# The masked cross-attention of a two-layer perceiver, written anew in the form of its sister, with fp32 probabilities and values

## The chip, the cores and the metric

The kernel runs on 1 core of one Trainium2 chip. The metric is the device time of one execution in microseconds (us). All six phases of the model are one program on that core: masked cross-attention (x0), a state-space layer (m0), a quantised feed-forward layer (f0), a sigmoid cross-attention (x1, here "the sister"), self-attention (a1) and routed experts (e1).

## What is computed

There are 128 batches of 32 tokens, width 256, and for each batch a context of 257 rows of width 256. The change touches the first phase only, whose reference is:

```python
q = _split_heads(query @ Wq + bq, B)
k = _split_heads(key @ Wk + bk, B)
v = _split_heads(value @ Wv + bv, B)
scores = jnp.einsum('bhqd,bhkd->bhqk', q, k) / np.sqrt(D_K)
scores = jnp.where(mask[:, None, :, :] > 0, NEG, scores)
p = jax.nn.softmax(scores, axis=-1)
x = jnp.einsum('bhqk,bhkd->bhqd', p, v)
x = x.transpose(0, 2, 1, 3).reshape(B, -1, D_MODEL)
return x @ Wo + bo
```

There are 16 heads of 16 columns; the query is the layer-normed residual stream, key and value are the context, the mask is int32 of shape 128 x 32 x 257, and NEG is -1e9. The result is added to the residual.

## The kernel before

The residual stream (4096 tokens x 256, fp32) stays in SBUF as `all_xres`, 32 tiles of 128 tokens. A tile is a **group** of four batches (`GB = 4`, `NT = 32` groups). The function `cross_attention` (L179) serves x0 alone (`soft` is true); the sister has a function of its own, `sigmoid_attention` (L976), which isn't touched.

An fp32 operand of a product is mostly kept as two fp16 tiles, hi and lo (hi is the value rounded, lo the rest), and `mm_split` makes three fp16 matmuls of one product: hi x hi, lo x hi, hi x lo (L263 is the line of all its matmuls, L1147 that of the sister's). In tile names h and l at the end are these halves; `x_psK`, `x_psV`, `x_psS`, `x_psT`, `x_psO` and `x_psM` are PSUM tiles for keys, values, scores, transposed probabilities, attention output and small things (psA, a part of psM, serves transposed queries, queries and output projection in turn).

What each engine does for a batch slot c (the numbers in brackets are lags, which keep the engines apart):

- **PE**: the transposes of batch c-2's probabilities, eight fp32 transposes of 128x128 (L464); values of c, twelve matmuls of 256 columns; scores of c, twelve of 256 columns over all 128 rows (the queries stand in a block-diagonal tile, `x_qbd`) and twelve of one column for context row 257; keys of c+1, twelve of 256 columns; then attend of c-2, 24 fp16 matmuls in 64-column tiles, and more for row 257. Once in four batches each: transposed and projected queries, keys and values of row 257, output projection.
- **DVE**: `softmax_max` (L843, four custom instructions that add the mask and take the row maximum, then `x_nm`, L846), the reciprocals of the row sums (L852), the lo halves of keys (L882), values (L890) and probabilities (L861, twice), extraction of the heads from psO, conversion of the mask (`to_add`, L829), the layer norm's last step (L174).
- **ACT**: four exponentials with row sums (L705), the hi halves of probabilities (L676), values (L697), keys (L689) and queries (L659).
- **POOL**: normalises the probabilities (L376, four a batch), splits the context in hi and lo (L346, L348), spreads the queries into `x_qbd` by a head mask of 8 columns (L356), copies row 257 (L332, L336), adds the output bias (L367).
- **SP** issues the loads: for each group the context (L299, 128 x 2056 fp32) and behind it four copies of the mask (L305).

The order of work is written by hand: every engine has its own loop over the batches, in program order, and engines meet in semaphores. An instruction whose semaphore isn't up holds everything behind it on its engine. Buffers: context 2 (a group each), keys 2, values 4, probabilities 2, transposed probabilities 1, mask int32 1 and converted 2.

Of the kernel before, what the change touches and what calls it, by code (L numbers as in the profile page):

```python
# [6 lines left out]
F32 = mybir.dt.float32  # L7
# [5 lines left out]
ALU = mybir.AluOpType  # L13
# [165 lines left out]
def cross_attention(nc, d, xres, con, norm, layer):  # L179

    soft = layer == 0
    with ExitStack() as ctx:
        sp = Space(nc, ctx, f"x{layer}")
        sb, ps, sem = sp.sb, sp.ps, sp.sem
        pre = f"L{layer}_xattn_"

        W = {k: (sb(f"w{k}h", [P, C, D], F16), sb(f"w{k}l", [P, C, D], F16)) for k in "qkvo"}
        begin_layer(nc, f"x{layer}w", xres, norm, [(d[pre + "W" + k], *W[k], WS) for k in "qkvo"])
        bq, bk, bv = (sb(f"b{k}", [P, C], F32) for k in "qkv")
        bo = sb("bo", [P, D], F32)
# [12 lines left out]
        V = [(sb(f"vh{n}", [P, C, 256], F16), sb(f"vl{n}", [P, C, 256], F16)) for n in range(4)]
        kx = [(sb(f"kxh{n}", [P, C, GB], F16), sb(f"kxl{n}", [P, C, GB], F16)) for n in range(2)]
        xk = (sb("xkh", [P, C, 96], F16), sb("xkl", [P, C, 96], F16))
        vx3 = sb("vx3", [96, D], F16)  # L210
        vxm = [sb(f"vxm{n}", [96, GB, D], F16) for n in range(2)]

        NP = 2
        prob = [sb(f"prob{n}", [P, 4, S2], F32) for n in range(NP)]
        pT32 = sb("pT32", [P, 4 * 256], F32) if not soft else None
        mx = [sb(f"mx{n}", [P, 4], F32) for n in range(2)]
        nm = [sb(f"nm{n}", [P, 4], F32) for n in range(2)]
        sm = [sb(f"sm{n}", [P, 4], F32) for n in range(2)]
        rs = [sb(f"rs{n}", [P, 4], F32) for n in range(2)]
        pT = [(sb(f"pTh{n}", [P, 2, 512], F16), sb(f"pTl{n}", [P, 2, 512], F16)) for n in range(1 if soft else 2)]  # L220
        px = [sb(f"px{n}", [P, 96], F32) for n in range(2)]
        px3 = sb("px3", [96, P], F16)

        oT = [sb(f"oT{n}", [P, GB, C, T], F32) for n in range(2)]
        ob = sb("ob", [P, C, P], F32)
        obp = (sb("obh", [P, C, P], F16), sb("obl", [P, C, P], F16))
# [3 lines left out]
        psA = psM[:, 0:256]  # L230
        psX = psM[0:96, 256:384]
        psKx = psM[:, 384:392]
        psSx = psM[:, 392:408]
        score = [psS, psS] if soft else [psS, psT]
        SC = 0.25 / (WS * WS)
        PXS = 1.0 if soft else PS

        const_in, bias_ready, px_zeroed = sem("const_in"), sem("bias_ready"), sem("px_zeroed")
        ctx_in = [sem(f"ctx_in{n}") for n in range(2)]
        mask_in, mask_used = sem("mask_in"), sem("mask_used")  # L240
        pool_passed, sync_passed = sem("pool_passed"), sem("sync_passed")
        ctx_hi, ctx_split, xk_hi, xk_ready = sem("ctx_hi"), sem("ctx_split"), sem("xk_hi"), sem("xk_ready")
# [3 lines left out]
        vx_mm, vx_hi, vx_lo, vxm_ready = sem("vx_mm"), sem("vx_hi"), sem("vx_lo"), sem("vxm_ready")  # L246
        k_mm, k_hi, k_lo = sem("k_mm"), sem("k_hi"), sem("k_lo")
        v_mm, v_hi, v_lo = sem("v_mm"), sem("v_hi"), sem("v_lo")
        s_mm, sx_taken, s_max, nm_ready, dve_passed = (sem(k) for k in ("s_mm", "sx_taken", "s_max", "nm_ready", "dve_passed"))
        exp_done, r_ready, p_norm = sem("exp_done"), sem("r_ready"), sem("p_norm")  # L250
        p_main = sem("p_main")
        t_mm, pt_hi, pt_lo, pv_mm = sem("t_mm"), sem("pt_hi"), sem("pt_lo"), sem("pv_mm")
        pxT_mm, px_hi, px_lo, o_full = sem("pxT_mm"), sem("px_hi"), sem("px_lo"), sem("o_full")
        o_part, o_ext, ob_ready, ob_hi, ob_lo = sem("o_part"), sem("o_ext"), sem("ob_ready"), sem("ob_hi"), sem("ob_lo")
# [4 lines left out]
        def mm_split(eng, out, lhs, rhs, start, stop, lint=False):  # L259

            prods = [p for a, b in zip(lhs, rhs) for p in split_products(a, b)]
            for n, (a, b) in enumerate(prods):
                last = eng.matmul(out, a, b, start=start and n == 0, stop=stop and n == len(prods) - 1,  # L263
                                  skip_group_check=lint)
            return last

        def both(pair, f):
            return (f(pair[0]), f(pair[1]))

        LASTI = NT // 2 - 1

        def run(eng, body):
            for i in range(LASTI + 1):
                body(i)

        def preps(i, gp):

            return not (isinstance(i, int) and i == LASTI and gp == 1)  # L280

        def started(i, c, lag):

            return not (isinstance(i, int) and 8 * i + c - lag < 0)


        @block.sync
        def _(sync):
            if soft:
                for t, k in ((bq, "q"), (bk, "k"), (bv, "v")):  # L290
                    sync.dma_start(t[:], d[pre + "b" + k]).then_inc(const_in, 16)
                sync.dma_start(bo[:], d[pre + "bo"].rearrange("(a n) -> a n", a=1).to_broadcast([P, D]))\
                    .then_inc(const_in, 16)

            def load(i, gp):
                g = i * 2 + gp
                wait_apart(sync, ctx_split, (g - 1) * GB, sync_passed)
                wait_apart(sync, xk_ready, g - 1, sync_passed)
                sync.dma_start(ctx32[gp][:], d["ctxT"][bass.ds(g, 1)].rearrange("a p j c s -> (a p) j c s"))\  # L299
                    .then_inc(ctx_in[gp], 16)  # L300
                if soft:
                    wait(sync, mask_used, g)
                    src = d["mask"][bass.ds(g * GB, GB)].rearrange("j q k -> q j k")
                    for h in range(4):
                        sync.dma_start(mraw[32 * h:32 * h + 32], src).then_inc(mask_in, 16)  # L305

            def body(i):
                for gp in range(2):
                    load(i, gp)
# [2910 lines left out]
```

## Time and profile before

| | before |
|---|---|
| median of 3 runs | 3196.28 us |
| the runs | 3201.59, 3191.54, 3196.28 us |
| the profiled execution | 3201.86 us |
| its span | 3200.1 us |
| mean granted TensorE clock | 0.923 of full |
| PE, DVE, ACT, POOL busy over the span | 85%, 72%, 60%, 60% |
| instructions | 85879 |

The span is the time from the first to the last record of the profile; the profiled execution is 1.8 us longer. The shares are means over six phases with different limits, so they say little of one phase; a window's row gives the same for a stretch of time. x0 lies between about 40 and 1045 us.

### The profile page before, as it was taken

To read this page: it belongs to the slowest core of one execution; us is meant where nothing else is said; L and a number is where in the kernel's file an instruction comes from. 1 tells how busy PE (TensorE), PEld (TensorE's weight loads), DVE (VectorE), ACT (ScalarE), POOL (GpSimd) and SP (SyncE) were. 2 spreads that over 40 slices of the span, in tenths; PEclk is the share of its full clock that TensorE was granted. 3 is DMA by queue.
4 is the path that set the end of the run, shared out by engine and by line. 5 is a ranking of instruction groups with operands and counts; after the bars stand their busy time and mean duration, and the time that the engine had idled before them with its cause. 6 is when DMAs were issued, how large, how long until landed. Compare 5 with 4: busy or idle time off the path is not lost. (4 is left out here: it accounts for less than half of the span.)

```text
span 3200.1 us, 85879 instructions
## 1 busy us (share of the span) xinstructions
PE 2706.9 (85%) x32700; PEld 2118.3 (66%) x32700; DVE 2312.3 (72%) x5209; ACT 1905.3 (60%) x4534; POOL 1931.9 (60%) x2135
## 2 busy tenths in 40 slices
PE   3999999999998489998677999999995788546998
PEld 2877777777777355555344788888884666434776
DVE  4999999999998387777634677777775788663443
ACT  2666767676666577767233677777773666343333
POOL 4888788888885477777300766666662677233332
PEclk9999999999999688988688999999997999757999
DMA  5121111111110000000000221111210000352110
GB/s 144 42 61 61 42 61 50 53 61 42 61 48 2 20 1 1 1 1 1 14 16 16 93 61 57 53 59 61 61 47 16 2 2 2 121 182 74 38 38 28
DMA packets 87375, 143.57 MB, mean 45 GB/s; under 512 B 10784, under 2 KB 74144, under 8 KB 80704
## 3 DMA queue, kind: packets, MB, share of 16 engines
q1 hardware_dynamic: 82304, 123.52, 12.4%
q0 software_dynamic: 4672, 14.57, 1.3%
q8 instruction: 270, 4.42, 0.6%
q14 instruction: 129, 1.06, 0.1%
HBM read 123.37 MB, written 14.69 MB: 43 GB/s over the span
## 5 line engine op out<-in xcount | busy, mean ns | idle before, releaser
L376 POOL TENSOR_SCALAR x_prob<-x_prob,x_rs 128x257 f32<-128x257 f32 x512 | 247.8, 484 | 173.1 <-DVE x_rs L852 141.6
L705 ACT ACTIVATE x_prob<-x_prob,x_nm 128x257 f32<-128x257 f32 x512 | 254.3, 498 | 152.6 <-DVE x_nm L846 152.5
L2119 DVE TENSOR_TENSOR_SCAN m_s<-m_a,m_psD 128x1024 f32<-128x1024 f32 x128 | 284.9, 2267 | 2.3 <-PE m_psD L1946 2.2
L1420 DVE SCALAR_TENSOR_TENSOR x_pTl<-x_psS,x_pTh 128x1024 f16<-128x1024 f32 x128 | 156.7, 1225 | 145.3 <-ACT x_pTh L1328 145.3
L843 DVE CUSTOM_DVE_ANT_0 x_prob<-x_psS,x_masked,x_prob 128x256 f32<-128x256 f32 x512 | 217.3, 481 | 4.5
L2058 ACT ACTIVATE m_a<-m_dt,m_rate 128x248 f32<-128x248 f32 x512 | 206.8, 492 | 0.0
L1108 POOL TENSOR_TENSOR x_qbdh<-x_qh,all_mask4h 128x1024 f16<-128x1024 f16 x32 | 60.6, 1895 | 217.5 <-DVE x_ql L1401 217.5
L1830 POOL TENSOR_TENSOR m_s<-m_s 128x1024 f32<-128x1024 f32 x64 | 150.5, 2352 | 67.8 <-DVE m_s L2119 67.8
L3003 ACT ACTIVATE e1t_g<-e1t_psH,e1t_bias 128x128 f32<-128x128 f32 x312 | 89.2, 368 | 171.0 <-PE e1t_psH L2952 171.0
L689 ACT ACTIVATE x_kh<-x_psK,x_bk 128x256 f16<-128x256 f32 x256 | 107.5, 471 | 118.6 <-PE x_psK L263 116.1
L861 DVE TENSOR_TENSOR x_pTl<-x_psT,x_pTh 128x512 f16<-128x512 f32 x256 | 164.2, 682 | 5.6 <-ACT x_pTh L676 3.0
L1341 ACT ACTIVATE x_vh<-x_psV 128x512 f16<-128x512 f32 x128 | 76.4, 597 | 134.7 <-PE x_psV L1147 134.7
L1100 POOL TENSOR_TENSOR x_ctxl<-x_ctx,x_ctxh 128x512 f16<-128x512 f32 x128 | 149.7, 1170 | 10.7
L348 POOL TENSOR_TENSOR x_ctxl<-x_ctx,x_ctxh 128x512 f16<-128x512 f32 x128 | 144.1, 1125 | 10.7
L2952 PE MATMUL e1t_psH<-e1t_xnh,e_wh 128*128 128x128 f16 x624 | 143.2, 229 | 2.8 <-issue 2.2
L1147 PE MATMUL x_psK<-x_ctxh,x_wkh 128*128 128x256 f16 x512 | 142.0, 277 | 3.4 <-POOL x_ctxl L1100 3.1
L263 PE MATMUL x_psS<-x_kh,x_qbdh 128*128 128x256 f16 x512 | 140.5, 274 | 4.4 <-POOL x_qbdl L356 4.3
L1322 ACT ACTIVATE x_psS<-x_psS 128x1024 f32<-128x1024 f32 x128 | 129.0, 1008 | 24.2 <-PE x_psS L1241 24.2
L464 PE MATMUL x_psT<-all_ident,x_prob 128*128 128x128 f32 x1024 | 135.8, 276 | 6.5 <-POOL x_px L382 6.5
L1147 PE MATMUL x_psV<-x_wvh,x_ctxh 128*128 128x256 f16 x512 | 141.0, 275 | 0.0
L1147 PE MATMUL x_psK<-x_ctxh,x_wkl 128*128 128x256 f16 x512 | 140.7, 275 | 0.0
L1147 PE MATMUL x_psK<-x_ctxl,x_wkh 128*128 128x256 f16 x512 | 140.7, 275 | 0.0
(599 smaller groups left out, 11913.9 us busy)
## 6 DMA issues: line engine op xcount, KB each, us to landing
x_ctx<-in_ctxT SPq DMA_DIRECT2D x32, 1028.0 KB, 6.3
x_ctx<-in_ctxT SPq DMA_DIRECT2D x32, 1024.0 KB, 5.9
x_mraw<-in_mask SPq DMA_DIRECT2D x128, 128.5 KB, 2.8
e1r_stage<-in_L_ffn_w SPq DMA_DIRECT2D x16, 1024.0 KB, 5.0
e_rows<-e1r_pad POOLq DMA_DIRECT2D x1, 5070.0 KB, 19.6
e1t_row<-e_rows SPq DMA_DIRECT2D x39, 130.0 KB, 2.1
all_xres<-in_x SPq DMA_DIRECT2D x1, 4096.0 KB, 14.2
x_vxr<-x_vx SPq DMA_DIRECT2D x128, 32.0 KB, 3.4
```

The lines of the kernel that those rows point to most:

```text
L348: pool.tensor_tensor(lo[:, j], src, hi[:, j], ALU.subtract).then_inc(ctx_split, 1)
L376: last = pool.tensor_scalar(prob[n][:, h, :], prob[n][:, h, :], rs[n][:, h:h + 1], PS, ALU.mult, ALU.mult)
L705: last = act.activation(prob[n][:, h, :], prob[n][:, h, :], ACT.Exp, bias=nm[n][:, h:h + 1], scale=SC, accum_out=sm[n][:, h:h + 1])
L843: dve.tensor_tensor_reduce(prob[n][:, h, 0:256], psS[:, h * 256:(h + 1) * 256], masked[gp][:, j, 0:256], 1.0, prob[n][:, h, 256:257], ALU. ...
L861: dve.tensor_tensor(pT[0][1][:, kt, :], psT[:, kt * 512:(kt + 1) * 512], pT[0][0][:, kt, :], ALU.subtract).then_inc(pt_lo, 1)
L1100: pool.tensor_tensor(lo[:, j], src, hi[:, j], ALU.subtract).then_inc(ctx_split, 1)
L1147: last = pe.matmul(out, a, b, start=m == 0, stop=m == len(prods) - 1)
L1420: dve.scalar_tensor_tensor(pT[c % 4][1][:].rearrange("p r k n -> p (r k n)"), psS[c % 2][:], PS, pT[c % 4][0][:].rearrange("p r k n -> p ( ...
L1830: pool.tensor_tensor(lower, lower, upper, ALU.add).then_inc(half_done, 1)
L2058: last = act.activation(A[k % 3][:, :, m, 1:T], dt[n % 2][:, h, :].rearrange("p (j t) -> p j t", t=T)[:, :, 1:T], ACT.Exp, scale=rate[:, h ...
L2119: dve.tensor_tensor_scan(states, rates, psD[at % 2][:], 0.0, ALU.mult, ALU.add).then_inc(scan_done, 1)
L2952: last = pe.matmul(bank[:, k % 4 * P:(k % 4 + 1) * P], a, b, start=m == 0, stop=m == len(prods) - 1)
```

## The change

`cross_attention` is replaced by `masked_attention` (L179 of the changed kernel); the other phases are as before. Its parts:

- **Loads.** Per group: `load_vx` (values of row 257, from DRAM, broadcast over partitions, 128 x 1024 fp32), `load_mask` (four copies), `load` (context without its last row, 128 x 8 x 256 fp32), in this order on SP. `load_vx(g)` waits for the `value_last` of batch 4g-5.
- **Row 257.** Its keys and values are computed for all 128 batches at the start (`last_keys`), its values go through a DRAM tensor `x0_vx`. Its scores are made once a group (`last_scores`), turned into the last column of the probabilities by `last_values` (DVE) and `place_last` (POOL), and its part of the output comes from `value_last` (POOL, `x_pv`) and four fp32 matmuls with the identity.
- **Softmax.** `minima` (DVE) works on -SC times the scores and takes the minimum, which is the exponential's bias, so `x_nm` isn't computed apart. The exponentials are not normalised: the row sums are spread (`spread_sums`, POOL), added up by two fp32 matmuls (`denominators`, PE), and the group's output is multiplied by the reciprocals (`normalise`, DVE). `mask` conversion moves from DVE to POOL (`to_add`).
- **Scores** run in two tiles of 64 rows, with the 4-column head mask.
- **Probabilities and values stay fp32**: their copies out of PSUM are whole (ACT and DVE take half of pT each, ACT takes V) and `attend` makes 8 fp32 matmuls of 64 columns instead of 24 fp16 ones. The products with Wq, Wk, Wv, Wo and the scores stay split.
- Buffers: keys and values 4, probabilities and transposed probabilities 3. Keys are made two batches ahead, attend lags by two.

The diff, cut to its core:

```diff
-def cross_attention(nc, d, xres, con, norm, layer):
+def masked_attention(nc, d, xres, con, norm):
+    NK, NV, NP, NW = 4, 4, 3, 3
...
-            def load(i, gp):
-                g = i * 2 + gp
-                wait_apart(sync, ctx_split, (g - 1) * GB, sync_passed)
...
+            def load(g):
+                wait(sync, ctx_split, (g - 1) * GB)
+                sync.dma_start(ctx32[g % 2][:], d["ctxT"][g][:, :, :, 0:LAST]).then_inc(ctx_in[g % 2], 16)
+            def load_mask(g):
+                wait(sync, mask_done, g)
...
+            def load_vx(g):
+                wait(sync, pv_last, (g - 1) * GB)
...
+            for g in range(NT):
+                load_vx(g)
+                if g > 0:
+                    load_mask(g)
+                if g > 1:
+                    load(g)
...
+            def to_add(g):
+                pool.wait_ge(mask_in, 64 * (g + 1))
...
+                pool.tensor_scalar(masked[g % 2][:], mraw[:, :, 0:LAST], 0.0, -BIG, ALU.is_gt, ALU.mult).then_inc(mask_done, 1)
+            def value_last(b):
+                g, j = b // GB, b % GB
+                pool.wait_ge(exp_done, b + 1)
+                pool.wait_ge(vxr_in[g % 2], 16 * (g // 2 + 1))
+                wait(pool, pv_mm, b - 1)
...
+            for b in SLOTS:
+                g, j = b // GB, b % GB
+                batch(value_last, b - 1)
+                if j == 2:
+                    group(spread, g + 1)
+                batch(split, b + GB)
+                if j == 0:
+                    group(spread_sums, g - 1)
+                    group(to_add, g + 1)
+                if j == 1:
+                    group(add_bo, g)
+                batch(place_last, b + 1)
...
+            for b in SLOTS:
+                g, j = b // GB, b % GB
+                batch(scores, b)
+                if j == 0:
+                    group(output, g - 2)
+                batch(keys, b + 2)
+                if j == 1:
+                    group(queries, g + 1)
+                if j == 2:
+                    group(denominators, g - 1)
+                if j == 3:
+                    group(last_scores, g + 1)
+                batch(turn, b - 1)
+                batch(values, b)
+                if j == 0:
+                    group(xnT, g + 1)
+                batch(attend, b - 2)
...
+            def minima(b):
+                g, j = b // GB, b % GB
+                dve.wait_ge(placed, b + 1)
+                dve.wait_ge(s_mm, b + 1)
...
+            for b in SLOTS:
+                g, j = b // GB, b % GB
+                batch(minima, b)
+                if b % 2 == 0 and 0 <= b - 4 < NB:
+                    extract((b - 4) // 2)
...
+                batch(take_pT, b - 1)
+                if j == 1:
+                    group(lo_q, g + 1)
+                    group(ln, g + 2)
+                batch(lo_k, b + 2)
```

ACT's loop of the new layer is exps(b), take_pT(b-1), [hi_q in a group's second slot], hi_k(b+2), take_v(b).

How the order of instructions moves, first on SP, whose queue carries all loads. Before, at the steady state of the layer:

```order
L299 DMA x_ctx_0<-in_ctxT 128x2056 [waits x0_xk_ready,x0_ctx_split]
L305 DMA x_mraw<-in_mask 32x4x257 [waits x0_mask_used]
L305 DMA x_mraw<-in_mask 32x4x257 x3
L299 DMA x_ctx_1<-in_ctxT 128x2056 [waits x0_xk_ready,x0_ctx_split]
L305 DMA x_mraw<-in_mask 32x4x257 [waits x0_mask_used]
L305 DMA x_mraw<-in_mask 32x4x257 x3
```

And SP after, at the same place (`x0_pv_last` is raised by `value_last`):

```order
L293 DMA x_vxr<-x_vx 128x1024 [waits x0_pv_last]
L288 DMA x_mraw<-in_mask 32x4x257 [waits x0_mask_done]
L288 DMA x_mraw<-in_mask 32x4x257 x3
L282 DMA x_ctx_0<-in_ctxT 128x8x256 [waits x0_ctx_split]
L293 DMA x_vxr<-x_vx 128x1024 [waits x0_pv_last]
```

The context load was the first of its group and depends only on the context's own users; it is now the last, behind the load that waits for `x0_pv_last`.

POOL in the first slot of a group, before (`x_xkh` and `x_xkl` are the halves of context row 257):

```order
L332 CAST x_xkh<-x_ctx_1 128x3x16 [waits x0_vx_mm,x0_ctx_in1]
L332 CAST x_xkh<-x_ctx_1 128x3x16
L336 TENSOR_TENSOR x_xkl<-x_ctx_1,x_xkh 128x3x16 [waits x0_xk_hi]
L336 TENSOR_TENSOR x_xkl<-x_ctx_1,x_xkh 128x3x16
L346 TENSOR_SCALAR x_ctxh<-x_ctx_1 128x512 [waits x0_v_mm,x0_ctx_in1]
L348 TENSOR_TENSOR x_ctxl<-x_ctx_1,x_ctxh 128x512 [waits x0_ctx_hi]
```

POOL in the first slot of a group, after:

```order
L350 TENSOR_TENSOR x_pv_1<-x_vxr,x_prob 128x256 [waits x0_pv_mm,x0_vxr_in1,x0_exp_done]
L316 TENSOR_SCALAR x_ctxh<-x_ctx_1 128x512 [waits x0_v_mm,x0_ctx_in1]
L318 TENSOR_TENSOR x_ctxl<-x_ctx_1,x_ctxh 128x512 [waits x0_ctx_hi]
L358 TENSOR_TENSOR x_sums<-x_eye_q,x_sm 128x512 [waits x0_sum_mm,x0_exp_done]
L336 TENSOR_SCALAR x_mlast<-x_mraw 128x4 [waits x0_last_done,x0_s_min,x0_mask_in]
L337 TENSOR_SCALAR x_masked<-x_mraw 128x1024
L343 COPY x_prob<-x_lastv 128x4 [waits x0_pv_last,x0_t_mm,x0_last_done]
```

Before, the split of the next group's first batch (L346, L348) followed the copies of row 257, and the normalisations of the running batch came after it. It (L316, L318) now stands right behind the `value_last` (L350) that SP's queue waits for, and the mask conversion (L337) and `place_last` (L343) stand behind the split.

PE after, at the end of one slot and the start of the next (attend, then scores; keys follow, waiting for `x0_k_lo` and `x0_ctx_split`):

```order
L512 MATMUL x_psO<-x_pT,x_v 64x128 [waits x0_pv_last,x0_pt_second,x0_o_ext,x0_pt_first,x0_v_out]
L512 MATMUL x_psO<-x_pT,x_v 64x128 x7
L518 MATMUL x_psO<-all_ident,x_pv_0 64x128 x4
L485 MATMUL x_psS<-x_kh,x_qbdh 128x256 [waits x0_s_min,x0_k_lo]
L485 MATMUL x_psS<-x_kh,x_qbdh 128x256
L485 MATMUL x_psS<-x_kl,x_qbdh 128x256 x2
L485 MATMUL x_psS<-x_kh,x_qbdl 128x256 x2
L485 MATMUL x_psS<-x_kh,x_qbdh 128x256 x2
L485 MATMUL x_psS<-x_kl,x_qbdh 128x256 x2
L485 MATMUL x_psS<-x_kh,x_qbdl 128x256 x2
L395 MATMUL x_psK<-x_ctxh,x_wkh 128x256 [waits x0_k_lo,x0_ctx_split]
```

An attend is now twelve products of 128 columns into tiles of 64 columns, and scores twelve in tiles of 64 rows.

## Rows read from the trace of the kernel before

**Rows 1.** Windows, 500 to 600 us (us, PE PEld DVE ACT POOL busy, PEclk, DMA, GB/s)
```profile
500.00:600.00 100.00, 92.72 (x1211) 78.75 (x1210) 91.64 (x274) 70.13 (x219) 82.20 (x120) 1.00 0.18 57
```

**Rows 2.** Waits of 300 to 900 us (us in total, times, longest)
```profile
ACT x_prob L705 <- DVE x_nm L846: 95.8, 79, 1.9
```

**Rows 3.** Timeline of DVE, the layer's first and last maximum (start us, us)
```profile
59.10 0.49 DVE L843 CUSTOM_DVE_ANT_0 x_prob<-x_psS,x_masked,x_prob 128x256 f32<-128x256 f32 x1
...
1028.32 0.48 DVE L843 CUSTOM_DVE_ANT_0 x_prob<-x_psS,x_masked,x_prob 128x256 f32<-128x256 f32 x1
```

**Rows 4.** Timeline of PE in x0, transposes and values
```profile
507.41 1.04 PE L464 MATMUL x_psT<-all_ident,x_prob 128*128 128x128 f32 x8
...
508.29 0.27 PE L263 MATMUL x_psV<-x_wvh,x_ctxh 128*128 128x256 f16 x1
508.40 0.27 PE L263 MATMUL x_psV<-x_wvl,x_ctxh 128*128 128x256 f16 x1
```

**Rows 5.** Timeline of PE in the sister, the scores' first and the keys' first
```profile
2000.55 0.23 PE L1241 MATMUL x_psS<-x_qbdh,x_kh 64*128 64x128 f16 x2
...
2001.33 0.28 PE L1147 MATMUL x_psK<-x_ctxh,x_wkh 128*128 128x256 f16 x1
```

**Rows 6.** Timeline of PE in the sister, an fp32 product beside fp16 ones
```profile
1910.56 0.43 PE L1186 MATMUL x_psM<-x_qx,x_head_sum 128*64 128x128 f32 x2
1910.72 0.24 PE L1261 MATMUL x_psO<-x_pTh,x_vh 128*64 128x128 f16 x1
...
1910.83 0.27 PE L1186 MATMUL x_psM<-x_qx,x_head_sum 128*64 128x128 f32 x1
```

**Rows 7.** The page's costliest groups, two of POOL (busy us, mean ns | idle before)
```profile
L376 POOL TENSOR_SCALAR x_prob<-x_prob,x_rs 128x257 f32<-128x257 f32 x512 | 247.8, 484 | 173.1 <-DVE x_rs L852 141.6
...
L1108 POOL TENSOR_TENSOR x_qbdh<-x_qh,all_mask4h 128x1024 f16<-128x1024 f16 x32 | 60.6, 1895 | 217.5 <-DVE x_ql L1401 217.5
```

**Rows 8.** Timeline of POOL in x0
```profile
515.89 0.62 POOL L346 TENSOR_SCALAR x_ctxh<-x_ctx 128x512 f16<-128x512 f32 x1
516.59 1.16 POOL L348 TENSOR_TENSOR x_ctxl<-x_ctx,x_ctxh 128x512 f16<-128x512 f32 x1
517.71 0.73 POOL L367 TENSOR_TENSOR all_xres<-all_xres,x_bo 128x256 f32<-128x256 f32 x1
```

**Rows 9.** Timeline of SP, one group's masks and the next context
```profile
525.67 1.75 SPq L305 DMA_DIRECT2D x_mraw<-in_mask  x4
527.51 0.38 SPq L299 DMA_DIRECT2D x_ctx<-in_ctxT  x1
```

**Rows 10.** The line of the context load, L299, all 32
```profile
DMA to landing us min/median/max: 4.8/6.3/10.8
```

**Rows 11.** Timeline of ACT in x0
```profile
523.84 0.51 ACT L705 ACTIVATE x_prob<-x_prob,x_nm 128x257 f32<-128x257 f32 x1 [1.23 <-DVE x_nm L846]
...
525.83 0.60 ACT L659 ACTIVATE x_qh<-x_psM,x_bq 128x128 f16<-128x128 f32 x2
526.33 1.06 ACT L676 ACTIVATE x_pTh<-x_psT 128x512 f16<-128x512 f32 x2
...
528.95 0.84 ACT L689 ACTIVATE x_kh<-x_psK,x_bk 128x256 f16<-128x256 f32 x2 [1.07 <-PE x_psK L263]
```

**Rows 12.** DVE: lo_k of x0 in its timeline, the norm's step in x0 and the sister
```profile
61.97 0.88 DVE L882 SCALAR_TENSOR_TENSOR x_kl<-x_psK,x_bk,x_kh 128x256 f16<-128x256 f32 x2 [0.24 <-ACT x_kh L689]
...
L174 DVE TENSOR_SCALAR x_xn<-all_xres,all_mean,all_rstd 128x256 f32<-128x256 f32 x29 | 11.7, 403 | 0.0
...
L174 DVE TENSOR_SCALAR x_xn<-all_xres,all_mean,all_rstd 128x256 f32<-128x256 f32 x32 | 41.9, 1310 | 0.0
```

**Rows 13.** Timeline of PE in the state-space layer, and a window right behind it
```profile
1157.76 0.39 PE L1946 MATMUL m_psD<-m_bd1h,m_ut1h 32*128 32x512 f16 x2 [2.48 <-DVE m_s L2119]
...
1159.60:1163.00 3.40, 3.40 (x19) 1.77 (x17) 3.09 (x3) 3.33 (x8) 3.04 (x2) 0.50 0.00 0
```

More of the change, by code:

```diff
@@ L219, in cross_attention @@
[L219 to L226, printed above, removed]
+        (xnp,), (qp,) = parts("xn", [P, C, P], 1), parts("q", [P, C, P], 1)
@@ L232, in cross_attention @@
[L232 to L242, printed above, removed]
+        psA, psX = psM[:, 0:256], psM[:, 256:272]
@@ L257, in cross_attention @@
         block = ctx.enter_context(nc.Block())
[L259 to L268, printed above, removed]
@@ L272, in cross_attention, with batch, group @@
[L272 to L284, printed above, removed]
+        SLOTS = range(NB + 2 * GB)
+        def batch(f, b):
+            if 0 <= b < NB:
+                f(b)
+        def group(f, g):
+            if 0 <= g < NT:
+                f(g)
@@ L430, in xnT @@
+            def xnT(g):
                 pe.wait_ge(norm_tile.done, g + 1)
+                wait(pe, x_done, g - 2)
+                wait(pe, last_done, g)
                 for c in range(C):
@@ new lines, in _ @@
+            for h in range(C):
+                for r in range(RG):
+                    rows = slice(64 * r, 64 * r + 64)
+                    last = act.activation(kxp[0][rows, h, r, :], psK[rows, h * NB:(h + 1) * NB], ACT.Identity,
+                                          bias=bk[rows, h:h + 1])
+            last.then_inc(kx_hi, 1)
+            act.wait_ge(vx_mm, 1)
+            act.activation(vx32[:], psV[:, 0:D], ACT.Copy).then_inc(vx_done, 1)
+            hi_xn(0)
+            hi_k(0)
+            hi_q(0)
@@ new lines, in _ @@
+            last.then_inc(kx_lo, 1)
+            lo_xn(0)
+            ln(1)
+            lo_k(0)
+            lo_q(0)
+            lo_k(1)
+            last_values(0)
+            for b in SLOTS:
+                g, j = b // GB, b % GB
+                batch(minima, b)
+                if b % 2 == 0 and 0 <= b - 4 < NB:
+                    extract((b - 4) // 2)
+                if j == 0:
+                    group(residual, g - 2)
+                if j == 2:
+                    group(normalise, g - 1)
+                if j == 3:
+                    group(last_values, g + 1)
+                batch(take_pT, b - 1)
+                if j == 1:
+                    group(lo_q, g + 1)
+                    group(ln, g + 2)
+                batch(lo_k, b + 2)
+                if j == 0:
+                    group(lo_xn, g + 1)
+                if j == 3:
+                    group(lo_ob, g - 1)
```

891 lines of the change are left out of this document (322 added, 569 removed).

## The prediction

> **What bounds the kernel now.** I read the windows first: in 500 to 600 us, inside the rewritten layer, PE and DVE are both busy over 90% of the time and TensorE's clock is full (PEclk 1.00) [rows 1]. The waits of 300 to 900 us name the cycle that paces a batch: scores, DVE's four maxima, nm, then ACT's exponentials, whose wait for nm is the longest in the list [rows 2]. The DVE timeline gives the layer's length. The first maximum of batch 0 starts at 59.10 us, that of batch 127 at 1028.32 us [rows 3], so the masked layer takes 969.2 us between them: 7.63 us a batch, 30.5 us a group of four. The other phases keep their code. The whole question is the new layer's group period.
>
> **The change where PE would be the bound.** Twelve 256-column matmuls of keys or of values take 12 x 0.11 = 1.31 us (the starts in rows 4 are 0.11 apart), the eight fp32 transposes of `turn` 0.88 (507.41 to 508.29) [rows 4]. The change keeps these 32 products of a batch, since weights, queries and keys stay split into fp16 halves; only probabilities and values become fp32. New per batch:
> - Scores: 12 matmuls in two 64-row tiles, six pairs, instead of 12 full ones and 12 of one column. The sister's 12 pairs of half the columns take 2000.55 to 2001.33 = 0.78 us [rows 5]; with the switch back I take 0.88.
> - Attend: 12 fp32 matmuls of 64-column tiles. The sister has such an fp32 product: its passes appear as rows of their own, 0.27 us apart with an fp16 matmul of the other half between them, 0.11 after the first of them [rows 6]. So a product is two passes of about 0.11, and if the halves overlap, 24 passes take 12 x 0.11 = 1.32, with switches 1.52.
>
> A bare slot is 0.88 + 1.31 + 0.88 + 1.31 + 1.52 = 5.9 us. Once a group come the output projection 0.65 and the queries 0.65 (half of 1.31 each), two transposes 0.22, the denominators 0.84 (two overlapping fp32 products of 256 columns, 0.44, and a tile switch of 0.2 on either side) and the last scores, at most 0.6: 3.0. That makes 4 x 5.9 + 3.0 = **26.6 us a group**, in slots of 6.8, 6.55, 6.75 and 6.5. DVE loses nm, the reciprocals, half of each pT and V; its new normalisation comes once a group. ACT and DVE hide under 26.6, and POOL, without its four 0.484 us multiplications a batch [rows 7], would too: its new list is about 2.7 us a batch (steps 1 and 3 below) and, a group, two spreads of 1.9 [rows 7], spread_sums, conversion and an add, some 19 us in all. Costed at nothing: the `mlast` column, `normalise` (two DVE operations a group, where DVE has room), and the start's keys and values of row 257, against which the old group-wise ones go.
>
> **The wait it adds.** SP now issues vx, four mask copies and then the context, and the vx load waits for `value_last` of the batch before the group's first slot, b0. On POOL the instruction behind that `value_last` is the split of batch b0+4, which needs this very context. Behind it stand spread_sums, the mask conversion (moved from DVE) and `place_last(b0+1)`, for which the minima of b0+1 wait. `value_last(b0-1)` itself waits for attend(b0-3), which ends where slot b0 starts on PE; call that 0. The case comes 30 times (groups 2 to 31 are loaded so).
> 1. `value_last`: 0.1 + 0.73, the duration of the 128x256 add in rows 8; hand-over to SP: **1.0**.
> 2. vx issue about 0.45, four masks 1.84 (525.67 to 527.51 [rows 9]): the context is issued at 3.3. Landing: a median of 6.3 us [rows 10] for a 1.03 MB load with 0.51 MB behind it. Now 0.51 + 0.51 MB go ahead of 1.02 MB. Scaled by bytes the whole burst takes 6.3 x 2.05/1.54 = 8.4 us from its first issue, so I take 6.0 from the context's: **9.3**. Bounds for this step: 4.8 (its fastest) and 8.4.
> 3. Split 0.62 + 1.16 = 1.8; spread_sums 1.16 (same shape and kind) [rows 8]; mlast 0.2; conversion of 128x1024 int32 on POOL, which no row shows. The bounds: twice the 0.62 of a 512-element tensor_scalar = 1.24, and four times 0.484 = 1.94 [rows 7]; I take 1.7, since the int32 source is the dearer-looking kind. place 0.2. The minima of b0+1 start at **14.4**.
> 4. From there: first minimum 0.49 [rows 3]; four exponentials 1.99 (523.84 to 525.83); half of the two pT copies, 0.53; hi_q 0.60; hi_k 0.84 [rows 11]; lo_k 0.88 [rows 12]; hand-overs 0.1: 5.4, so lo_k(b0+3) is ready at **19.8**. psK has one buffer, so keys(b0+4) on PE wait for it.
>
> Without the wait these keys would start at 6.8 + 6.55 + 0.88 = 14.2. The stall is 5.6 us, in two pieces of about 2.8 around scores(b0+2). After it come 1.31 + 0.84 + 0.88 + 1.31 + 1.52 = 5.86 and slot three, 6.5: the next group's zero is at **32.2**.
>
> The clock: after 2.48 us idle in the state-space layer PE ran at 0.50, 1.2 instead of 2.4 GHz, for 3.4 us, starting 1.8 us later [rows 13]. That is 1.7 us of work lost. Two gaps longer than that one follow each other here; I take one such stretch a group, bounds 0 and 2.5. Period **33.9**.
>
> Between lo_q and lo_k DVE also has ln of group g+2. In this layer that row is 0.40 us and hides beside hi_k; in the sister the same instruction means 1.31 [rows 12]. I take 0.40; 1.31 would add 0.9 us a group, 27 in all, and is the upper bound. The Trainium skill (page "SBUF — State Buffer", section "Who interferes with whom") says that VectorE and GpSimd share a port pair under an exclusive lock, so that one can block the other's whole instruction. By that rule 3314 rather than 3287 if POOL's `spread`, released as lo_q ends, is first at the port; the trace's two means agree with the rule, not with a fixed price.
>
> The Trainium skill also gives, for the SWDGE path ("DMA: Bandwidth & Descriptors", section "Anatomy of one DMA — SWDGE (gpsimd) path"), about 2.0 us plus bytes/436e9 for one transfer. An estimate by it for 2.05 MB is 6.7 us instead of my 8.3, which would make the sum 1.6 x 30 = 48 us less, 3239; our queue is SP's, and the medians of rows 10 are slower than that formula.
>
> **The sum.** Group 0 26.6, thirty groups 33.9 each = 1017.0, three last slots 20.1: 1063.7 against 969.2, or +94.5. Head and tail: the pipeline drains one stage sooner, about -4, bounds -14 and +6. Together +90. The profiled execution took 3201.9, giving 3292; the median of the runs is 5.6 below the profiled one, so the forecast is **3287 us**.
>
> **The rivals.**
> - *The fp32 halves do not overlap.* No row shows two fp32 products side by side. Then attend is 1.32 dearer; in slots 0 and 1 the stall covers it, in 2 and 3 it is 2.64, and the denominators 0.43: 3.07 x 30 = 92, with some 10 for the groups without a stall: **3389**. Against it speaks the spacing in rows 6. Chance 0.10.
> - *The stall never reaches PE* (the other side). If the burst lands and POOL finishes before PE has used up its keys, 31 x 26.6 + 20.1 = 844.7, which is -124.5, with -4: **3068**. The place is keys(b0+4). It decides on the period: at (969.2 + 4 - 46.7)/30 = 30.88 us the change costs nothing, so stall and clock together must come to less than 4.3 of my 7.3 for any gain. Against it: all four steps are serial, and rows give most of them. Chance 0.14.
> - *My chain with its cheap ends.* Landing -1.2, conversion -0.46, no clock loss -1.7 give 30.5: just no change, 3187. The dear ends (+2.4, +0.24, +0.8, ln +0.9) give 38.2: 3417. This is inside my main case.
> - *Another wait*, such as attend's for `value_last` or psM's sharing between five users, chance 0.08, either sign.
>
> **How the numbers follow.** Main case 0.68, of which 0.06 is faster and 0.02 the same; no overlap 0.10, slower; hidden 0.14, faster; the rest 0.08: 0.02 faster, 0.01 same, 0.05 slower. Faster by over 0.3% 0.22, within 0.3% 0.03, slower 0.75; 0.3%, some 10 us, is about what measuring this kernel can tell from no change. The range is 3170 to 3400: from the cheap ends with the head's bound to the no-overlap case. It leaves out the hidden case and the farthest dear ends.
>
> **What would show it.** Right: POOL idle before the split's first instruction (`ctxh`) on the context's DMA, about 8 us, 30 times; PE idle before keys (on lo_k) and before scores (on the minima), near 5.6 us a group; PEclk below 1.00 in the layer's windows; DVE far below 92%. Attend's 24 passes within 1.5 us show the overlap. Wrong: the context landing before `value_last` ends, or PE near 100% with a period under 28 us; or attend near 2.8 us.

## The result, and the profile after

| | before | after |
|---|---|---|
| median | 3195.06 us (4 runs) | 3414.5 us (4 runs, 3409.01 to 3417.94) |
| ratio | 1 | 1.0683, 95% interval 1.066 to 1.0705 |
| the profiled execution | 3201.86 us | 3414.86 us |
| mean granted TensorE clock | 0.923 | 0.882 |
| PE, DVE, ACT, POOL busy | 85%, 72%, 60%, 60% | 80%, 59%, 53%, 52% |

The changed kernel is slower by 219 us where +90 was forecast: the sign and the mechanism were right, the size was not, and the time lies outside the range.

The waits of 300 to 900 us after the change, which answer to [rows 2] (us in total, times, longest):

```profile
ACT x_prob L579 <- DVE x_nm L666: 266.7, 63, 13.4
DVE x_prob L666 <- POOL x_prob L343: 192.5, 16, 12.7
POOL x_ctxh L316 <- DMA x_ctx<-in_ctxT: 167.4, 16, 11.2
...
PE x_psS L485 <- DVE x_nm L666: 112.0, 16, 7.7
...
PE x_psK L395 <- DVE x_kl L679: 32.5, 15, 2.2
```

These are the links of the predicted chain, all but the first once a group (16 groups fall into the stretch): POOL's split waits 10.5 us for the context, DVE's minima 12.0 for `place_last`, PE 7.0 for the minima and 2.2 for lo_k. So PE is idle 9.2 us a group; the forecast had 5.6.

One group on POOL, from its timeline (start, duration, and in brackets the idle time before):

```profile
586.14 0.62 POOL L316 TENSOR_SCALAR x_ctxh<-x_ctx 128x512 f16<-128x512 f32 x1 [11.03 <-DMA x_ctx<-in_ctxT]
586.84 1.15 POOL L318 TENSOR_TENSOR x_ctxl<-x_ctx,x_ctxh 128x512 f16<-128x512 f32 x1
587.95 1.07 POOL L358 TENSOR_TENSOR x_sums<-x_eye_q,x_sm 128x512 f32<-128x512 f32 x1
588.99 0.25 POOL L336 TENSOR_SCALAR x_mlast<-x_mraw 128x4 f32<-128x4 int32 x1
589.30 3.63 POOL L337 TENSOR_SCALAR x_masked<-x_mraw 128x1024 f32<-128x1024 int32 x1
592.99 0.19 POOL L343 COPY x_prob<-x_lastv 128x4 f32<-128x4 f32 x1
```

From the split to `place_last` it is 7.04 us instead of 5.1, and the difference is the mask conversion, 3.63 us where I took 1.7. Before, DVE did it (four columns more):

```profile
L829 DVE TENSOR_SCALAR x_masked<-x_mraw x32: 683/686/2380, 50.4 to 982.3; 128x1028 f32<-128x1028 int32 x32
```

One group on SP, behind a `value_last` that starts at 614.01:

```profile
614.66 0.34 SPq L293 DMA_DIRECT2D x_vxr<-x_vx  x1
615.05 1.86 SPq L288 DMA_DIRECT2D x_mraw<-in_mask  x4
616.95 0.55 SPq L282 DMA_DIRECT2D x_ctx<-in_ctxT  x1
```

The line of the context load, all 32, which answers to [rows 10]:

```profile
DMA to landing us min/median/max: 6.2/7.8/8.8
```

SP issues as predicted, at once when `value_last` ends, with the context 2.3 us behind (in a third of the groups up to 1.5 us more, as the masks take longer to issue). But it then takes a median of 7.8 us to land, where it took 6.3 before and I took 6.0.

What it does to PE and its clock stands in windows of one group, which answer to [rows 1] (us, PE PEld DVE ACT POOL busy, PEclk, DMA share, GB/s):

```profile
587.49:595.06 7.57, 0.01 (x1) 0.03 (x1) 1.85 (x9) 1.32 (x5) 7.37 (x8) 0.73 0.00 0
595.06:598.70 3.64, 1.47 (x13) 0.85 (x14) 2.32 (x7) 3.21 (x11) 3.10 (x5) 0.50 0.01 2
598.70:602.40 3.70, 3.70 (x17) 1.92 (x17) 2.43 (x11) 2.08 (x8) 3.62 (x4) 0.50 0.02 4
602.40:604.40 2.00, 2.00 (x12) 1.88 (x11) 1.85 (x2) 0.00 (x0) 0.92 (x2) 0.50 0.00 0
604.40:607.26 2.86, 2.86 (x36) 2.32 (x35) 1.80 (x4) 1.92 (x4) 0.00 (x0) 0.96 0.00 0
607.26:613.76 6.50, 6.50 (x94) 5.60 (x94) 3.53 (x13) 4.75 (x16) 2.55 (x4) 1.00 0.02 5
```

The clock falls inside the first gap and is still at the lower of its two levels (0.50) when work comes back; it recovers near 604.4. The rest of the third slot, from the keys at 598.70 to the end of attend at 607.26, takes 8.56 us against the 5.86 of my sum. The group shown is one of the dearest: over 29 groups (102 to 1206 us, from the starts on PE's timeline) this stretch takes 7.62 us in the mean, 7.02 to 8.61. The last row is the fourth slot, at the predicted 6.5.

The first and the last minimum, from the line of `minima` (durations min/median/max, first and last start):

```profile
L666 DVE CUSTOM_DVE_ANT_0 x_prob<-x_psS,x_masked,x_lastv x512: 469/480/486, 59.0 to 1243.4; 128x256 f32<-128x256 f32 x171
```

The last of four instructions starts at 1243.4, so batch 127's first one at 1242.2 (they are 0.40 apart). The layer takes 1183.2 us instead of 969.2 [rows 3]: +214.0, and the profiled executions differ by 213.0. All of the change lies between these rows. With 26.6 for group 0 and 20.1 for the last slots the period is (1183.2 - 46.7)/30 = 37.9 us, forecast 33.9. From slot to slot on PE's timeline it is 38.0 (the same 29 groups, 36.7 to 38.9).

### The profile page after: what moved, and what is told of

Same layout as the page of the kernel before. It is cut to its first block and busy times, and to the rows that moved or that the text cites. A ratio compares the mean times of both kernels' runs of the same rounds, so it can differ in the third digit from the quotient of the medians.

```text
span 3413.0 us, 81224 instructions
## 1 busy us (share of the span) xinstructions
PE 2719.5 (80%) x31182; PEld 2093.3 (61%) x31182; DVE 2019.6 (59%) x4446; ACT 1806.0 (53%) x4252; POOL 1758.3 (52%) x1653
## 5 line engine op out<-in xcount | busy, mean ns | idle before, releaser
L666 DVE CUSTOM_DVE_ANT_0 x_prob<-x_psS,x_masked,x_lastv 128x256 f32<-128x256 f32 x512 | 216.9, 479 | 427.3 <-POOL x_prob L343 366.6
L485 PE MATMUL x_psS<-x_kh,x_qbdh 64*128 64x256 f16 x512 | 79.9, 304 | 211.8 <-DVE x_nm L666 211.8
L316 POOL TENSOR_SCALAR x_ctxh<-x_ctx 128x512 f16<-128x512 f32 x128 | 78.9, 616 | 323.7 <-DMA x_ctx<-in_ctxT 323.7
L395 PE MATMUL x_psK<-x_ctxh,x_wkh 128*128 128x256 f16 x512 | 157.5, 308 | 70.9 <-DVE x_kl L679 68.2
L350 POOL TENSOR_TENSOR x_pv<-x_vxr,x_prob 128x256 f32<-128x256 f32 x128 | 79.4, 620 | 222.7 <-PE x_psO L518 222.7
L485 PEld LDWEIGHTS x_psS<-x_kh,x_qbdh 64*128 64x128 f16 x512 | 28.2, 100 | 237.3 <-issue 231.4
L395 PE MATMUL x_psK<-x_ctxh,x_wkl 128*128 128x256 f16 x512 | 158.3, 309 | 0.0
L395 PE MATMUL x_psK<-x_ctxl,x_wkh 128*128 128x256 f16 x512 | 158.3, 309 | 0.0
L318 POOL TENSOR_TENSOR x_ctxl<-x_ctx,x_ctxh 128x512 f16<-128x512 f32 x128 | 148.2, 1158 | 10.7
L922 PE MATMUL x_psK<-x_ctxh,x_wkh 128*128 128x256 f16 x512 | 142.0, 277 | 3.8 <-POOL x_ctxl L875 3.4
## 6 DMA issues: line engine op xcount, KB each, us to landing
all_xres<-in_x SPq DMA_DIRECT2D x1, 4096.0 KB, 14.4
```

The source lines that it names most:

```text
L318: pool.tensor_tensor(lo[:, j], src, hi[:, j], ALU.subtract).then_inc(ctx_split, 1)
L395: last = pe.matmul(out, a, b, start=m == 0, stop=m == len(prods) - 1)
L666: dve.tensor_tensor_reduce(prob[b % NP][:, s, 0:LAST], psS[:, s * LAST:(s + 1) * LAST], masked[g % 2][:, j, :], -SC, lastv[g % 2][:, j, s: ...
L922: last = pe.matmul(out, a, b, start=m == 0, stop=m == len(prods) - 1)
```

## The experiments

Theory A is the prediction's: the order on SP's and POOL's queues makes a chain through the context's landing, and PE stands behind it. The rivals are written with each run. All ratios are against the kernel before, run on the same chip.

**e1, loads first.** The context and the masks go ahead of the load that waits for `value_last`.

```diff
             for g in range(NT):
-                load_vx(g)
-                if g > 0:
-                    load_mask(g)
                 if g > 1:
                     load(g)
+                if g > 0:
+                    load_mask(g)
+                load_vx(g)
```

> Theory A (the chain SP - context landing - POOL - minima - lo_k sets the group): context and masks are now queued ahead of the load that waits for value_last, so they are there a group early. Minima of b0+1 can start 7.8 us after the slot's start (0.7 value_last, 1.8 split, 1.1 sums, 0.25 + 3.63 conversion, 0.2 place) instead of 17.8, keys(b0+4) are ready at 13.3 and are wanted at 14.0: no stall, group period about 26.4 instead of 38.0, total 3414 - 30 x 11.6 = 3067 us (3040 to 3110), POOL's wait for the context gone. Theory B (the time lies in the fp32 products and TensorE's clock, the wait only fills room that another one would take, e.g. value_last against attend): period stays over 34, total above 3290.

Measured: 3090.72 us, ratio 0.9671 (0.9653 to 0.969), inside the range and 24 us over the 3067 expected. Its window of 500 to 600 us:

```profile
500.00:600.00 100.00, 96.65 (x1184) 80.69 (x1183) 71.95 (x215) 68.04 (x211) 69.92 (x81) 1.00 0.23 68
```

No instruction was taken away, five lines changed places, and 324 us are gone. PE is busy at 97% with its clock at 1.00, and POOL's wait for the context is out of the list. Theory A holds and B falls: the new form without the wait is 105 us *faster* than before.

**e2, the context alone first.** As e1, but with masks last, behind the vx load.

```diff
             for g in range(NT):
-                load_vx(g)
-                if g > 0:
-                    load_mask(g)
                 if g > 1:
                     load(g)
+                load_vx(g)
+                if g > 0:
+                    load_mask(g)
```

> Only the context goes ahead; vx and masks still wait for value_last. Theory A: masks land 6 to 7.3 us after the slot's start, conversion ends at 10 to 11.3, place, then 5.5 to lo_k: 15.6 to 16.9 where 14.0 is wanted, stall 1.6 to 2.9 and 0 to 1.7 of clock: total 3115 to 3205, between e1 and the changed kernel. Theory B: as e1, above 3290.

Measured: 3233.45 us, 1.0119 (1.0099 to 1.0138), 28 us above the range expected. Most of these 28 us are e1's own: the range was built on 3067 for e1, which took 3091. The wait moves to the masks:

```profile
602.80 0.24 POOL L336 TENSOR_SCALAR x_mlast<-x_mraw 128x4 f32<-128x4 int32 x1 [3.90 <-DMA x_mraw<-in_mask]
```

POOL goes on 7.4 us after `value_last`'s start (595.41), just over my upper end of 7.3, and the clock falls too (PEclk 0.91 and 0.93 in this kernel's windows of 300 to 400 and 500 to 600 us, 1.00 in e1's). Asking for the masks' 0.5 MB only when they are needed costs 143 us against e1, where I had 48 to 138.

**e3, the mask's conversion back on DVE.** The call leaves POOL's loop (first slot of a group) and comes into DVE's, behind lo_k of the third slot.

```diff
                     group(spread_sums, g - 1)
-                    group(to_add, g + 1)
...
                     group(lo_xn, g + 1)
+                if j == 2:
+                    group(to_add, g + 1)
```

> Loads in the changed kernel's order, but the mask's conversion is back on DVE (0.69 us there), at the end of the group's third slot. Theory A: POOL's chain is shorter by 3.9 us, all of it on the path: period 38.0 to 34.1, or 33.1 if the clock recovers too: 3267 to 3297 us. Theory B (landing alone or PE alone decides): within 20 us of 3414.

Measured: 3294.45 us, 1.0322 (1.0296 to 1.0349), inside the range and 120 us under the changed kernel. On POOL, `place_last` now follows `spread_sums` at once:

```profile
604.68 1.07 POOL L351 TENSOR_TENSOR x_sums<-x_eye_q,x_sm 128x512 f32<-128x512 f32 x1
605.69 0.19 POOL L336 COPY x_prob<-x_lastv 128x4 f32<-128x4 f32 x1
```

30 x 3.9 is 117, so the conversion lay on the path with its full length. The clock gave nothing back: from the third slot's keys to the end of its attend it is 7.7 us here (29 groups), 7.6 in the changed kernel.

**e4, `place_last` ahead of the split.**

```diff
+                batch(place_last, b + 1)
                 batch(split, b + GB)
...
-                batch(place_last, b + 1)
```

> POOL's place_last goes ahead of the split, so minima(b0+1) no longer stand behind the context. Theory A: the wait doesn't vanish but moves one batch on: place_last(b0+2) stands behind the conversion that ends at 17.8, minima(b0+2) start at 18.6, lo_k(b0+4) ends at about 25, keys(b0+5) were wanted at 20.7: stall 4.4 and some clock, period near 32.5, total 3200 to 3300. If the context were needed by the keys themselves (theory C: PE waits for the split, not for the minima), no gain: 3400 or more.

Measured: 3222.92 us, 1.0102 (1.0077 to 1.0128), inside the range. POOL still waits for the context as long as before, so theory C falls: PE did not wait for the split itself. The waits of 300 to 900 us show where the rest went:

```profile
POOL x_ctxh L316 <- DMA x_ctx<-in_ctxT: 192.8, 19, 11.1
DVE x_prob L666 <- POOL x_prob L343: 103.5, 33, 6.1
...
PE x_psO L512 <- DVE x_oT L686: 61.9, 19, 4.2
```

The minima now wait up to 6.1 us instead of 12.7, and the long wait is one batch further on, as expected. But PE meets this wait in another place than I said: attend waits 3.3 us a group for the extraction on DVE, which stands behind the late minima, before any keys do.

**e9, the context first, but all behind `value_last`.** This separates the place in the burst from the wait.

```diff
             for g in range(NT):
-                load_vx(g)
-                if g > 0:
-                    load_mask(g)
+                wait(sync, pv_last, (g - 1) * GB)
                 if g > 1:
                     load(g)
+                if g > 0:
+                    load_mask(g)
+                load_vx(g)
```

> As the changed kernel, all loads still wait for value_last, but the context is the first of them, then masks, then vx. This isolates what the place within the burst costs. The context should land about 6.3 us after its issue (the median with the masks behind it before) and at 7.4 after the slot's start instead of 10.7; split, sums and conversion end at 14, minima 3.5 us earlier than now, period 38.0 to 34.5, or 33.5 with less clock loss: 3280 to 3310 us. If the transfers' bandwidth alone counts (masks then land last, and the conversion waits for them), less than 60 us are gained: 3355 or more.

Measured: 3310.37 us, 1.0356 (1.0337 to 1.0375), at the upper edge of the range. The line of the context load:

```profile
DMA to landing us min/median/max: 5.6/6.4/9.7
```

At the head of the burst the landing is 6.4 us, nearly [rows 10]; behind vx and masks 7.8. So the load's place in the burst costs 1.4 us of landing and 2.3 of issue, 3.7 x 30 = 111 us; 104 were measured. e9 and e1 differ only in the wait for `value_last`, which costs the other 220 us.

**e6, attend by halves.** On e1's base; the loops over the halves r go outside, so neighbouring products use the same 64 columns of the array.

```diff
-                for kt in range(2):
-                    for c in range(C):
-                        to = (c * 2 + b % 2) * P
-                        for r in range(RG):
+                for r in range(RG):
+                    for kt in range(2):
+                        for c in range(C):
+                            to = (c * 2 + b % 2) * P
...
```

The four products with the identity are turned in the same way.

> e1 with attend's products ordered by half: all of the upper 64 output rows first, then the lower, so that neighbours use the same half of the array. If two fp32 products of different halves overlap (my main case), attend's 24 passes take 24 x 0.11 = 2.64 instead of 1.32 us and each batch is 1.2 us longer on PE, which is the bound: 3091 + 128 x 1.2 = 3245 us (3200 to 3260). If they never overlapped, no change: 3091.

Measured: 3134.06 us, 0.9802 (0.9783 to 0.9822): 43 us over e1, not 154, and so between my two readings and outside the range. Attend of one batch on PE in e1, then in e6:

```profile
604.21 1.09 PE L512 MATMUL x_psO<-x_pT,x_v 128*64 128x128 f32 x16
605.13 0.61 PE L518 MATMUL x_psO<-all_ident,x_pv 128*64 128x128 f32 x8
605.67 0.28 PE L485 MATMUL x_psS<-x_kh,x_qbdh 64*128 64x256 f16 x2
```

```profile
604.21 1.25 PE L512 MATMUL x_psO<-x_pT,x_v 128*64 128x128 f32 x13
605.20 0.32 PE L518 MATMUL x_psO<-all_ident,x_pv 128*64 128x128 f32 x1
605.30 0.27 PE L512 MATMUL x_psO<-x_pT,x_v 128*64 128x128 f32 x1
605.36 0.27 PE L518 MATMUL x_psO<-all_ident,x_pv 128*64 128x128 f32 x1
...
606.16 0.28 PE L485 MATMUL x_psS<-x_kh,x_qbdh 64*128 64x256 f16 x2
```

From attend's start to the next scores it is 1.46 us in e1 (my 1.52) and 1.95 in e6. Sixteen passes in 0.92 us (604.21 to 605.13), where the 0.11 of an fp32 pass in [rows 4] would make 1.76, show that the halves overlap in e1. Neighbours in different halves matter, but this order takes away only part of the overlap: in e6 the second half's last products of L512 run between the first half's of L518. The order costs 0.49 us a batch, 63 us in all; 43 show in the time, because e1's wait for lo_k (see e8) shrinks from 0.84 to 0.3 us a group. How a fully serial attend would do stays open.

**e7, the fp16 halves back.** On e1's base; probabilities and values are split again (ACT makes both hi parts, DVE both lo parts of pT and the lo of V), attend has 24 fp16 matmuls, row 257 stays fp32.

```diff
-                        for r in range(RG):
-                            s = r * C + c
...
+                        for vh, ph in ((0, 0), (1, 0), (0, 1)):
+                            for r in range(RG):
+                                s = r * C + c
...
-                dve.tensor_copy(pT[b % NW][:, 1, :], psT[:, 512:1024]).then_inc(pt_second, 1)
+                for kt in range(2):
+                    last = dve.tensor_tensor(pT[b % NW][1][:, kt, :], psT[:, kt * 512:kt * 512 + 512], pT[b % NW][0][:, kt, :],
+                                             ALU.subtract)
+                last.then_inc(pt_second, 1)
...
+                batch(lo_v, b)
```

> e1 with probabilities and values split into fp16 halves again (24 fp16 matmuls instead of 8 fp32 ones in attend; row 257 stays fp32). On PE 12 x 0.055 = 0.66 instead of 8/12 of 1.32 = 0.88 us, 0.2 less a batch: by PE alone 3091 - 28 = 3063. But DVE gets 1.3 us a batch more (two subtractions of 0.65 instead of one copy of 0.69, and the value's 0.68), ACT 0.5, and lo_k stands behind it: DVE rises from 72% to about 90%, psV and psT are freed later. I expect the second to win: 3110 to 3180. If PE alone decides: near 3063.

Measured: 3123.61 us, 0.9772 (0.9754 to 0.9791): 33 us slower than e1. Its window of 500 to 600 us:

```profile
500.00:600.00 100.00, 90.39 (x1260) 74.97 (x1256) 83.13 (x239) 69.88 (x216) 68.44 (x76) 1.00 0.26 81
```

A line of its waits of 300 to 900 us, and under it attend's first and the next scores' first row on PE's timeline:

```profile
PE x_psK L395 <- DVE x_kl L691: 49.5, 43, 1.2
```

```profile
604.30 0.25 PE L513 MATMUL x_psO<-x_pTh,x_vh 128*64 128x128 f16 x2
...
605.53 0.28 PE L485 MATMUL x_psS<-x_kh,x_qbdh 64*128 64x256 f16 x2
```

The split attend is shorter on PE (1.23 us against 1.46), but DVE goes from 72 to 83% and PE waits for lo_k in two slots of a group. So PE gains nothing from fp32 here; it costs PE 0.23 us a batch and pays on DVE.

**e8, `normalise` later.** On e1's base, DVE's `normalise` goes behind pT and lo_k.

```diff
-                if j == 2:
-                    group(normalise, g - 1)
...
                 batch(lo_k, b + 2)
+                if j == 2:
+                    group(normalise, g - 1)
```

> e1, and on DVE the group's normalise (1.76 + 0.43 us) comes after pT and lo_k instead of before. In e1 PE still waits 0.84 us before the keys of the group's last slot, for lo_k, which stands behind normalise. If that is the cause, 31 x 0.84 = 26 us less: 3065 (3055 to 3080). If the wait comes from the minima further up, within 8 us of 3091.

Measured: 3065.17 us, 0.9592 (0.9574 to 0.9611), as expected to the microsecond; the fastest kernel of this study, 4.1% under before and 10.2% under the changed one. Its window:

```profile
500.00:600.00 100.00, 100.00 (x1214) 83.87 (x1213) 71.58 (x225) 69.89 (x220) 75.72 (x83) 1.00 0.29 86
```

In e1 PE waited once a group for lo_k; in e8's list of 300 to 900 us this line is gone:

```profile
PE x_psK L395 <- DVE x_kl L679: 18.4, 22, 0.8
```

The line of `minima` in e8:

```profile
L666 DVE CUSTOM_DVE_ANT_0 x_prob<-x_psS,x_masked,x_lastv x512: 470/480/486, 59.0 to 889.1; 128x256 f32<-128x256 f32 x171
```

PE has no gap left: this is the PE-bound form that the prediction's first part costed.

**e10 and e11, the split in e8's order.** Both are e8 with e7's edit. e10 also puts the keys' halves ahead of the probabilities', on DVE as below and on ACT with hi_k likewise; e11 doesn't.

```diff
-                batch(take_pT, b - 1)
...
                 batch(lo_k, b + 2)
+                batch(take_pT, b - 1)
```

> e8 with probabilities and values split again, and with the keys' halves ahead of the probabilities' on ACT and DVE (the probabilities have a slot of slack, the keys none). It asks whether the split form lost in e7 by its own cost or by standing in front of lo_k. In e7 attend took 1.23 us instead of 1.46, but PE waited 1.1 us for lo_k in two slots of a group. If only the place mattered, PE is at 100% again and each batch is 0.23 us shorter: 3065 - 128 x 0.23 = 3036 (3030 to 3050). If DVE's added 1.3 us a batch is too much wherever it stands (83% busy in e7), 3065 or more.

> e8 with probabilities and values split, nothing else moved (e10 moved the keys' halves too, and PE then waited for the output projection's lo half, 46 us of 600). Compared with e8 (3065) it gives what the split costs in the better order; with e7 (3124, the split in e1's order) what the later normalise gives here. If DVE's extra 1.3 us a batch is the price, it stays 35 to 80 us above e8: 3100 to 3145. If the split only lost through lo_k standing behind normalise, it falls to 3065 or below.

Measured: e10 3142.08 us, 0.9817 (0.9796 to 0.9837); e11 3196.68 us, 1.0011 (1.0001 to 1.0021). e10 is in the second of its two cases (3065 or more), 77 us over e8. e11 missed its range by 52 us: the order that saved 26 us with fp32 costs 73 with the split (e7 to e11). The waits of 300 to 900 us in e11:

```profile
DVE x_pTl L678 <- ACT x_pTh L589: 135.9, 78, 2.3
...
PE x_psM L395 <- DVE x_obl L713: 41.9, 19, 2.2
```

DVE waits 1.7 us in every batch (78 times in the stretch) for ACT's hi half of the probabilities, with lo_k behind it, and PE waits 2.2 us a group for the output's lo half: `normalise` now delays the next minima, and with them the exponentials, ACT's hi half and all that stands behind it on DVE. With fp32 copies ACT and DVE take their halves of psT independently.

The waits alone don't explain the times. A group is 2.3 us longer in e11 than in e7 (from the first minimum to the last it is 964.4 us against 893.6), but PE waits only 0.9 us more in it (3.6 against 2.7). The rest goes with the clock. The stretch right behind a gap of 2.2 us in e11, and e11's window:

```profile
604.66:607.82 3.16, 3.16 (x15) 2.24 (x16) 3.09 (x13) 2.08 (x8) 3.10 (x3) 0.50 0.86 264
...
500.00:600.00 100.00, 88.93 (x1163) 71.73 (x1162) 77.26 (x217) 62.21 (x193) 62.29 (x71) 0.95 0.22 65
```

e7's gaps are at most 1.2 us and its clock stays at 1.00. e10 has the gap of 2.2 us too, waits no more than e7 in sum (2.6 us a group), and is still 18 us slower, at 0.98. So the split loses 33 us in one order and 131 in the other, and I can't say what it would lose in an order made for it; that part of "the split costs DVE time" is shown only for these three orders.

## Why the prediction was right, and where it was wrong

- **The mechanism** was right at every link: the order on SP, the context's landing, POOL's split, the conversion, the minima, lo_k, the keys. e1 undoes it with the loads' order alone.
- **The steps that failed** are 2, the landing, and 3, the conversion; both were too cheap in the sum. In its own terms, us from the start of the slot b0 on PE, means of the groups' starts on the timelines of POOL, SP, DVE and PE (30 groups; 29 for the slots):

| | forecast | measured |
|---|---|---|
| the context is issued | 3.3 | 3.5 |
| it has landed, the split starts (step 2) | 9.3 | 11.4 |
| the minima of b0+1 start (step 3) | 14.4 | 18.4 |
| keys(b0+4) start (step 4) | 19.8 | 23.9 |
| from there to the third slot's end, with the clock | 5.86 + 1.7 | 7.6 |
| the fourth slot | 6.5 | 6.5 |
| the period | 33.9 | 38.0 |

- **The landing (step 2)** was mis-sized by 2.1 us a group. I scaled [rows 10] by bytes and took 6.0 from the context's issue; it is 7.8, and the issue itself comes 0.2 later. The bounds (4.8 to 8.4) held the median. e9 shows 1.4 us of it as the load's place behind 1 MB.
- **The conversion (step 3)** was mis-sized by 1.9 us a group: 1.7 taken, bounds 1.24 to 1.94, measured 3.63. No row showed POOL with an int32 source, and both bounds came from fp32 rows, so they bounded nothing. On DVE the same work was 0.69 before; I priced a move between engines by the new engine's rate for another type. e3 confirms the 3.9 with its mlast column.
- **Step 4**, from the minima to the keys, was 5.4; it is 5.5 (in the group shown 593.21, first minimum on DVE, to 598.70). `ln` is 0.40 in the changed layer, as taken:

```profile
L174 DVE TENSOR_SCALAR x_xn<-all_xres,all_mean,all_rstd x32: 401/404/1017, 39.6 to 1169.1; 128x256 f32<-128x256 f32 x32
```

The shared-port rule (the Trainium skill, "SBUF — State Buffer", "Who interferes with whom") would have made it the dearer one if `spread` came first. Here `ln` follows lo_q and starts before `spread`, 597.36 against 597.52 in the group above, and isn't held up; so it is in 30 of the layer's 32 cases. The other order occurs in e4, where `ln` starts while POOL is splitting a context:

```profile
599.86 1.16 POOL L318 TENSOR_TENSOR x_ctxl<-x_ctx,x_ctxh 128x512 f16<-128x512 f32 x1
...
600.04 1.14 DVE L174 TENSOR_SCALAR x_xn<-all_xres,all_mean,all_rstd 128x256 f32<-128x256 f32 x1
```

POOL's operation ends at 601.02 and `ln` at 601.18, and so it goes in the groups where they meet this way: in e4 `ln` takes 0.40 to 1.26 us, 0.74 in the median. The rule holds there, and 1.31 was no fixed price.

- **The stall**: forecast 5.6, measured 7.0 + 2.2 = 9.2 of idle time, and the scores between the two gaps, at the lower clock, take 0.7 us more. The landing and the conversion account for 4.0 of these 4.3 us.
- **The clock**: I took 1.7, bound 2.5, from one stretch behind a 2.48 us gap [rows 13]. In the mean this was right (7.62 - 5.86 = 1.8), but the single groups lie between 1.2 and 2.8. In the group shown, behind gaps of 7.6 and 2.2 us, the lower level lasted until 604.4, with 5.7 us of work on the path (3.70 + 2.00) in it, and the slot was longer by 2.7.
- **PE's own work**: 26.6 a group was forecast; e8, with PE always busy, starts batch 0 at 59.0 and the last batch at 887.9, so a group is (828.9 - 20.1)/31 = 26.1. Half a microsecond less than the parts' sum.
- **The sum** now reads 23.9 + 7.6 + 6.5 = 38.0, where it read 33.9. Thirty times 4.1 is 124 us. Group 0 and the last slots took 4.7 us less than forecast, and head and tail gave -1 instead of -4; so the profiled execution's +213 exceeds my +90 by 123.
- **The rivals.** The hidden stall (3068) didn't happen; but e8 and e1 give 3065 and 3091, so as a price for the kernel without the wait it was right. The halves overlap, as the main case had it; what the rival would have cost stays open, since e6 is only in part serial.
- **The range** ended at 3400, though the prediction's own dear ends add up to 3417, just over the measured 3414.5. It would have been luck to be covered by them: they hold 0.9 us for `ln` and 0.8 for the clock that didn't come, and only 0.24 for the conversion, which needed 1.93.

## What to carry to other kernels

A load's time is set by what stands ahead of it in its queue and by that one's wait, so give each transfer whose buffer is free early a place ahead of one that waits late; here five lines turned a loss of 219 us into a gain of 105. When an instruction moves to another engine, its type conversion needs a row of that engine with those types; a row of the same shape in fp32 is no bound. And after a gap count the clock as well: the work behind the stalls ran at half speed for several microseconds, and one gap of 2.2 us (e10) cost more than three smaller ones of about the same sum (e7).

## What the runs showed of the hardware

- A tensor_scalar from int32 to fp32 of 128x1024 takes 3.63 us on POOL, in all 32 cases within 0.02; DVE did 128x1028 of it in 0.69. The POOL operation from fp32 to fp16 of half the size takes 0.62.
- A POOL multiplication of 128x256 fp32 with a broadcast operand took 0.62 us where the addition of the same shape took 0.73.
- DVE's reciprocal of 128x256 fp32 out of PSUM took 1.76 us, and with the 0.43 us product behind it, in front of lo_k, it was enough to hold PE for 0.8 us a group in e1.
- Twelve fp32 products of 64 columns, 24 passes of 128, take 1.46 us from the first to what follows them when neighbours alternate between the array's halves (e1), and 1.95 when ordered by half (e6).
- Behind PE gaps of 2.2 us in e11 the granted clock was 0.50 for 1 to 3.4 us; behind e7's gaps of up to 1.2 us it stayed at 1.00.
- DVE's `ln` (128x256 fp32) took 0.40 us when it started 0.16 before a POOL multiplication of 128x1024, and up to 1.26 (e4) when one of POOL's subtractions was under way.
- The issue of the same four mask copies on SP took 1.86 us in one group, 3.11 in another, and 4.26 in one of e9; what stands behind them is issued that much later.
